# A graph layer on one core: a transposition moved on TensorE, two waits moved to ScalarE, a full-height last chunk and an earlier first message

## The reference, cut to what matters

```
h   = relu(layernorm(x))                       # x: 50000 x 128, float32
xn  = layernorm(h) * g1 + b1
msg = relu(xn[src] + edge_attr)                # 25000 edges, sorted by dst
aggr = segment_sum(msg, dst, 50000)
u   = (1 + eps) * xn + aggr
u   = relu(u @ Wg1 + bg1) @ Wg2 + bg2          # the GIN part, 128 -> 128 -> 128
h2  = h + u
f   = gelu(layernorm(h2)*g2+b2 @ Wf1 + bf1) @ Wf2 + bf2    # 128 -> 512 -> 128
out = x + h2 + f
```

## Time and profile before

| | |
|---|---|
| three runs, us | 1043.13, 1045.61, 1047.68 |
| profiled execution, us | 1042.96 |
| its span, us | 1041.2 |
| TensorE busy | 982.8 us, 94% |
| VectorE busy | 965.1 us, 93% |
| ScalarE busy | 852.8 us, 82% |
| GpSimd busy | 825.9 us, 79% |

### The profile page before, as it was taken

How to read it: one execution, slowest core, us unless ns; L and a number is a source line. 1 busy time by engine, 2 the same in 40 slices (tenths; PEclk the granted TensorE clock), 3 DMA queues, 4 the chain that set the end, 5 groups by cost and what they waited for, 6 DMA issues and landing times. The chain is left out here.

```text
span 1041.2 us, 23085 instructions
## 1 busy us (share of the span) xinstructions
PE 982.8 (94%) x6684; PEld 857.0 (82%) x6684; DVE 965.1 (93%) x3499; ACT 852.8 (82%) x2158; POOL 825.9 (79%) x510
## 2 busy tenths in 40 slices
PE   1569999999999999999999999999999999999978
PEld 0357888988889889889888889889889889888867
DVE  5979999999999999999999999999999999998642
ACT  1458888898888988988888988988988988978853
POOL 7788888888788888888888888888888888876610
PEclk9869999999999999999999999999999999999999
DMA  7856766877886654555654664654654554543221
GB/s 259 228 165 162 204 172 179 242 230 220 253 238 157 160 130 118 157 133 117 156 135 116 154 139 116 157 136 115 158 134 116 150 140 117 125 105 81 51 60 41
DMA packets 110468, 156.87 MB, mean 151 GB/s; under 512 B 24835, under 2 KB 50607, under 8 KB 110334
## 3 DMA queue, kind: packets, MB, share of 16 engines
q1 hardware_dynamic: 70358, 128.99, 39.0%
q0 software_dynamic: 37760, 25.66, 17.7%
q10 hardware_dynamic: 2216, 0.66, 0.3%
HBM read 90.61 MB, written 64.61 MB: 149 GB/s over the span
## 5 line engine op out<-in xcount | busy, mean ns | idle before, releaser
L451 POOL DMA_INDIRECT aggr_sums<-e_merged,e_index x196 | 339.2, 1731 | 80.6 <-issue 70.7
L939 PE MATMUL p_out<-wf,n_act 128*128 128x128 f32 x3136 | 370.5, 276 | 1.6
L939 PEld LDWEIGHTS p_out<-wf,n_act 128*128 128x128 f32 x3136 | 357.7, 191 | 6.9 <-DVE p_out L855 5.9
L460 POOL TENSOR_TENSOR n_rstd<-n_var,minus_half 128x16 f32<-128x16 f32 (+3 forms) x102 | 259.7, 2557 | 48.3 <-DVE n_var L835 32.2
L532 ACT ACTIVATE n_act<-p_f,bf1e_col 128x512 f32<-128x512 f32 x392 | 256.2, 680 | 35.2 <-PE p_f L902 31.3
L440 POOL DMA_INDIRECT e_x<-in_x,e_cols x196 | 223.2, 1139 | 61.0 <-issue 59.4
L902 PE MATMUL p_f<-n_z2T_high,wf_low 128*128 128x512 f32 x392 | 202.0, 515 | 5.6 <-DVE n_z2T_low L701 4.8
L902 PE MATMUL p_f<-n_z2T_high,wf_high 128*128 128x512 f32 x392 | 155.1, 396 | 0.0
L902 PE MATMUL p_f<-n_z2T_low,wf_high 128*128 128x512 f32 x392 | 154.6, 394 | 0.0
L687 DVE BATCH_NORM_STATS2 n_stat<-n_x 128x6 f32<-128x256 f32 x392 | 140.3, 418 | 0.6 <-issue 0.4
L614 ACT ACTIVATE n_inT<-p_in 128x512 f32<-128x512 f32 x98 | 58.5, 597 | 99.0 <-PE p_in L946 99.0
(11 more groups left out here) (85 smaller groups left out, 1455.4 us busy)
## 6 DMA issues: line engine op xcount, KB each, us to landing
n_x<-in_x SPq DMA_DIRECT2D x97, 256.0 KB, 3.0
n_aggr<-aggr_sums SPq DMA_DIRECT2D x97, 256.0 KB, 2.7
out_dram<-n_out SPq DMA_DIRECT2D x97, 256.0 KB
aggr_sums<-zeros SPq DMA_DIRECT2D x26, 512.0 KB, 5.2
e_dst<-in_dst_rows SPq DMA_DIRECT2D x49, 256.0 KB, 3.8
e_attr<-in_attr SPq DMA_DIRECT2D x48, 256.0 KB, 3.5
aggr_sums<-zeros SPq DMA_DIRECT2D x12, 1024.0 KB, 5.7
e_x<-in_x,e_cols POOLq DMA_INDIRECT x196, 3.7
```

The source lines that it names most:

```text
L451: nc.gpsimd.indirect_dma_start(out=aggr, out_offset=bass.IndirectOffsetOnAxis(ap=e_index[0:r, s, j:j + 1], axis=0), in_=e_merged[0:r, s, j ...
L460: return nc.gpsimd.tensor_tensor(n_rstd[0:r, s, lo:hi], n_var[0:r, s, lo:hi], minus_half[0:r, 0:(hi - lo) * J].rearrange("p (a j) -> p a j ...
L939: last = nc.tensor.matmul(p_out[0:b.rows, j, :], n_act[:, k, j, 0:b.rows], wf2[:, k, :], start=False, stop=(k == KF - 1), skip_group_check ...
```

## The change

- On TensorE the transposition of z2 now stands between `p_g` and FFN1's quarters 2 and 3, not behind them.
- `merged_rows` on ScalarE takes over two waits of GpSimd in the branch that is taken: for the zeroed parts of `aggr_sums` and for the scatters of the chunk before. GpSimd's wait for `s_eindex` goes too.
- The last chunk's gathers and scatters always take 128 partitions. VectorE first fills the chunk's index rows from 96 on with spare rows beyond the sums (one copy of 32 partitions by 4), then writes the 106 true ones.
- `FIRST_JOINED` is 2: the powers of chunks 2 and 3 go into those of blocks 0 and 2 (in column 2, where nothing else stands so early), so those two node powers are 12 columns wide instead of 8, and two powers of their own disappear.
- In the prologue ScalarE makes a chunk's message one step earlier (`messages(edge(2))`); there, that is chunk 0.

```diff
-        FIRST_JOINED = 4
+        FIRST_JOINED = LEAD - 1
+        def joined_column(c):
+            return 3 if block_beside(c) >= 3 else 2
...
             def gather(c, columns):
-                r, s = c.rows, c.slot(3)
+                s = c.slot(3)
...
-                        out=e_x[0:r, s, j, :], out_offset=None, in_=x,
+                        out=e_x[0:P, s, j, :], out_offset=None, in_=x,
...
             def scatter_pair(c, g):
-                            ap=e_index[0:r, s, j:j + 1], axis=0),
-                        in_=e_merged[0:r, s, j, :], in_offset=None,
+                            ap=e_index[0:P, s, j:j + 1], axis=0),
+                        in_=e_merged[0:P, s, j, :], in_offset=None,
...
                     pool.wait_ge(s_emerged, c.at + 1)
-                    pool.wait_ge(s_eindex, c.at + 1)
+                    if apart:
+                        pool.wait_ge(s_eindex, c.at + 1)
...
-                    if not apart:
-                        for q in s_zeroed[zeroed_for(c.k - 1) if c.k else 0:zeroed_for(c.k)]:
-                            pool.wait_ge(q, 32)
-                    if not c.is_number(0):
+                    if apart and not c.is_number(0):
                         pool.wait_ge(q_scatter[(c.k - 1) % 3], SCATTERED * (c.value + (c.k - 1) // 3 + 1))
...
-                    power(b.rows, b.slot(8), 0, 4 if with_chunk else 3 if together else 2).then_inc(s_nrstd, 1)
+                    power(b.rows, b.slot(8), 0, 2 + together + with_chunk).then_inc(s_nrstd, 1)
...
+            def messages(c):
+                if c is not None:
+                    act.wait_ge(s_esum, c.at + 1)
+                    reached(act, s_emm, c.at - 2)
+                    nc.scalar.activation(e_msg[0:c.rows, c.slot(3)], e_sum[0:c.rows, c.slot(3)],
+                                         ACT.Relu).then_inc(s_emsg, 1)
-            def merged_rows(c):
+            def merged_rows(c, apart):
                 if c is not None:
+                    if not apart:
+                        for q in s_zeroed[zeroed_for(c.k - 1) if c.k else 0:zeroed_for(c.k)]:
+                            act.wait_ge(q, 32)
+                        if not c.is_number(0):
+                            act.wait_ge(q_scatter[(c.k - 1) % 3], SCATTERED * ((c.k - 1) // 3 + 1))
                     act.wait_ge(s_emm, c.at + 1)
...
-                if 0 in halves and (c := edge(3)) is not None:
-                    act.wait_ge(s_esum, c.at + 1)
...
+                if 0 in halves and not alone(node, apart):
+                    messages(edge(3))
+                elif 1 in halves and alone(node, apart):
+                    messages(edge(2))
...
+                    if r < P:
+                        lo = r // 32 * 32
+                        nc.vector.tensor_copy(e_index[lo:P, s], spare[lo:P]).then_inc(s_spare_rows, 1)
+                        dve.wait_ge(s_spare_rows, 1)
...
-                if (b := seventh) is not None:
-                    first_product(b, (2, 3))
                 if (b := sixth) is not None:
                     pe.wait_ge(s_z2, b.at + 1)
                     reached(pe, s_z2T_low, b.at)
                     ...
                     last.then_inc(s_tz2, 1)
+                if (b := seventh) is not None:
+                    first_product(b, (2, 3))
```

More of the change, by code:

```diff
@@ L219, in gnn_kernel @@
              "order_in", "bounds", "order", "bad", "flag"))
+        s_spare_rows = sem("s_spare_rows")
         s_zeroed = [sem(f"s_zeroed{i}") for i in range(len(ZERO_PARTS))]
@@ L440, in gather @@
                     nc.gpsimd.indirect_dma_start(
-                        out=e_x[0:r, s, j, :], out_offset=None, in_=x,
-                        in_offset=bass.IndirectOffsetOnAxis(ap=e_cols[0:r, s, 0, j:j + 1], axis=0),
+                        out=e_x[0:P, s, j, :], out_offset=None, in_=x,
+                        in_offset=bass.IndirectOffsetOnAxis(ap=e_cols[0:P, s, 0, j:j + 1], axis=0),
                         bounds_check=bound,
@@ L497, in step @@
                     if with_chunk:
-                        assert together and block_beside(c) == b.k
+                        assert together == (joined_column(c) == 3) and block_beside(c) == b.k
                         pool.wait_ge(s_evar, c.at + 1)
-                    power(b.rows, b.slot(8), 0, 4 if with_chunk else 3 if together else 2).then_inc(s_nrstd, 1)
+                    power(b.rows, b.slot(8), 0, 2 + together + with_chunk).then_inc(s_nrstd, 1)
                 if ending is not None and not together:
@@ L575, in step @@
                 if 1 in halves and 0 not in halves and (c := edge(3)) is not None and not c.is_number(0):
-                    merged_rows(c)
+                    merged_rows(c, apart)
                 if (b := node(0)) is not None:
@@ L587, in step @@
                     gelu(b, 3)
-                if 0 in halves and (c := edge(3)) is not None:
-                    act.wait_ge(s_esum, c.at + 1)
-                    reached(act, s_emm, c.at - 2)
-                    nc.scalar.activation(e_msg[0:c.rows, c.slot(3)], e_sum[0:c.rows, c.slot(3)],
-                                         ACT.Relu).then_inc(s_emsg, 1)
+                if 0 in halves and not alone(node, apart):
+                    messages(edge(3))
+                elif 1 in halves and alone(node, apart):
+                    messages(edge(2))
                 if (b := node(5)) is not None:
@@ L774, in second_half @@
                     dve.wait_ge(s_estatu, c.at + 1)
-                    to = n_var[0:r, block_beside(c) % 8, 3] if joined(c, apart) else e_var[0:r, s, 1]
+                    to = n_var[0:r, block_beside(c) % 8, joined_column(c)] if joined(c, apart) else e_var[0:r, s, 1]
                     nc.vector.scalar_tensor_tensor(to, e_stat[0:r, s, 1, :, 2], 1.0 / D, e_var[0:r, s, 0],
@@ L799, in sum_of @@
                         dve.wait_ge(s_nrstd, block_beside(ending) + 1)
-                        rstd = n_rstd[0:r, block_beside(ending) % 8, 3]
+                        rstd = n_rstd[0:r, block_beside(ending) % 8, joined_column(ending)]
                     else:
```

## The result

Three rounds on one chip, each kernel in turn: after 1034.43 us (median of 6 runs, 1033.29 to 1037.35), before 1046.46 us (6 runs, 1043.13 to 1047.77). The ratio is 0.9891, with a 95% interval from 0.9872 to 0.9911: 11 to 12 us faster, with an interval from 9.3 to 13.4. The profiled execution of after took 1033.71 us, span 1031.9; that of before 1042.96 and 1041.2. Between the two profiles lie only 9.3 us, since the one of before was among its fastest runs.

A forecast was written before the change was run, and what follows sets the result against it. VectorE and the loop of power, scatters, landing and load of sums bound the middle; the last chunk's slow scatters, the end. 7.0 + 2.1 + 0.85 + 1.5 = 11.4 us less gave 1034, range 1029 to 1039.5.

The forecast's parts named there:

- Part 1: Last chunk's scatters on 128 partitions land like the others; the 16.0 us step returns to 9.0: 7.0 us less.
- Part 2: Last chunk's gathers on 128 partitions: VectorE's n_in near 909 us no longer waits for late sums, 2.1 us less.
- Part 3: Transposition of z2 on TensorE: hidden in waits of three of the last steps, 0.85 us less; nothing in the middle.
- Part 4: Prologue: earlier message and joined powers bring forward gathers VectorE awaits near 57 and 75 us; 1.5 us less.
- Part 5: Two waits moved from GpSimd to ScalarE's e_merged: cost 0, and GpSimd's saved time goes unused, so 0.
- A: Last chunk's scatters stay slow, their landing due to its rows or the program's end: 1043 us; chance 0.07.
- B: Middle gets faster too, through GpSimd's saved time (1028 us) or the weight loads' waits (1013 us); chance 0.08.
- C: ScalarE is held by the moved wait, slower than before: 1086 us at 1.1 us in each of 47 pairs; chance 0.04.
- D: The tail's gain comes, but prologue and gathers give nothing: 1038 us; chance 0.11.

The follow-up runs named there:

- last chunk alone: The kernel before with 128 partitions in the last chunk's gathers and scatters, and the copy of spare rows, alone: 1031.77 us, ratio 0.9908.
- waits alone: The kernel before with the two waits moved from GpSimd to ScalarE's e_merged and GpSimd's wait for s_eindex removed: 1042.76 us, ratio 1.0005.
- order alone: The kernel before with only the transposition of z2 moved ahead of FFN1's quarters 2 and 3: 1040.79 us, ratio 0.9991.
- prologue alone: The kernel before with only the powers of chunks 2 and 3 joined to the blocks' and chunk 0's message a step earlier: 1041.25 us, ratio 0.9997.
- scatters 128: The kernel before with 128 partitions in the last chunk's scatters only, its gathers still on 106: 1038.24 us, a single run.
- 112: The kernel after with 112 partitions instead of 128 in the last chunk's gathers and scatters: 1035.47 us, a single run.
- 122: The kernel after with 122 partitions instead of 128 in the last chunk's gathers and scatters: 1044.96 us, a single run.
- one zero later: The kernel after with one zeroing transfer put off by a step, the one at 35.8 us instead of the intended one at 50.4: 1035.48 us.
- attributes 128: The kernel after with the last chunk's loads of e_attr and e_cols over 128 partitions too: 1035.05 us, ratio 0.9881 to the kernel before.

## Why the prediction was right

The forecast was 1034 and the measured median is 1034.43. The likeliest case was the one that came, and the parts priced at 9.95 of its 11.45 us measured 10.2 below. The last 1.5, the prologue's, aren't borne out. Without them the same sum gives 1035.7, which the measurement doesn't tell from 1034.2 either; that the total fits to half a microsecond is luck.

One pair of profiles can't price parts of 1 to 2 us: between before and the last chunk alone, which run the same code in the middle, the middle alone differs by 5.0 us (766.79 and 761.80). The experiments give several profiles for each side of every part, so the steps are read as means between fixed points: VectorE's first read of gathered rows (e_stat), and the starts of TensorE's `p_g` in steps 7, 90 and 98 (us from the span's start):

```
                 prologue  gathers  transp.  scatters   e_stat   step 7  step 90  step 98  span
before           old       106      old      106         14.63    89.81   906.28   984.91  1041.2
waits alone      old       106      old      106         15.36    91.21   905.21   983.74  1040.9
order alone      old       106      new      106         15.38    91.04   902.93   982.43  1039.0
prologue alone   new       106      old      106         14.49    88.71   903.92   982.60  1039.2
scatters 128     old       106      old      128         15.33    91.35   907.76   987.09  1036.4
last chunk 128   old       128      old      128         15.23    91.10   902.70   979.80  1029.2
after            new       128      new      128         14.42    89.37   906.02   983.36  1031.9
112              new       112      new      112         14.51    89.82   908.43   985.20  1033.7
122              new       122      new      122         14.23    89.28   906.25   985.86  1043.2
one zero later   new       128      new      128         14.56    89.60   908.34   985.25  1033.7
attributes 128   new       128      new      128         14.15    88.82   904.31   981.09  1029.7
```

(In the second row the start of step 7 is taken from the end of its `p_g`, whose first part the trace lacks.)

- **Part 1, the last chunk's scatters: 7.0 predicted.** From step 98 to the end, old order: 56.29, 57.16 and 56.60 us with 106, 49.31 and 49.40 with 128. Means 56.68 and 49.36: **7.3**. The mechanism held at each point: the landing took 3.4 us at most for the 3.8 assumed, n_in came at 985.27, TensorE did not wait. The slowest landing of the earlier trace rows (7.0), the lower bound's, did not come. That the partitions are the cause was an estimate, from this chunk's being the one on 106; the runs with 112 and 122 show it (3.1 us at most and 8.05). That same 7.0 speaks against one reason given: "no other of the 192" scatters was slow isn't so, since one in the middle took as long as chunk 48's.
- **Part 2, its gathers: 2.1 predicted.** From step 90 to step 98: 78.63, 78.53, 79.50, 78.68 and 79.33 with 106, and 79.61 with 122; 77.10, 77.34, 76.77, 76.91 and 76.78 with 128 or 112. Means 79.05 and 76.98: **2.1**. The pair of profiles had shown 1.3 over this stretch and 1.6 over the one step. The copy of the spare rows takes 0.36 us (at 932.47 in after), for the 0.3 that was kept, and costs nothing that is seen. The size held, the path only in part. In before and in the waits alone the loads of the sums land late, after up to 4.8 and 5.0 us, and n_in waits 2.20 and 2.35. With 128 or 112 they take 3.2 at most, and n_in's wait in after is 0.54 (at 909.30). But with 122 no load beside the gathers took more than 3.1, and the time was lost to the gathered rows themselves:

```profile
922.73 0.77 DVE L701 BATCH_NORM_STATS2 e_stat<-e_x 106x6 f32<-106x256 f32 x2 [2.50 <-DMA e_x<-in_x,e_cols]
```

  The same wait is 1.98 us in the order alone and 1.22 with the scatters on 128; it doesn't appear with 128 or 112. The prediction had no term for it. GpSimd's issues of the chunk's gathers also take 1.64 to 1.70 us with 106 and 1.75 to 1.81 with 122, for 1.04 to 1.26 in after, and what that adds isn't separated.
- **Part 3, the transposition: 0.85 predicted.** From step 98 to the end with fast scatters: 49.31 and 49.40 old; 48.54, 48.50, 48.45 and 48.61 new. Means 49.36 and 48.52: **0.8**. In the middle nothing, as argued: a wait of 0.3 us of the weight loads was one that TensorE's 1.39 us groups covered. Beside the slow scatters the same span shows no gain (56.57 and 57.34 with the new order), but the gain is there. From the start of the next step's FFN2 to the end of the last one it is 32.37 to 32.39 us in all five kernels with the old order, and 31.53 to 31.58 in all six with the new. What covers it is the stretch ahead of that FFN2, behind TensorE's standstill (5.23 us in before, 4.88 in the order alone, 4.87 and 5.17 in the prologue and the waits alone, 6.42 with 122): from p_in it takes 7.20 us in before, 7.80 and 8.07 in the prologue and the waits alone, 7.91 with 122 and 8.46 in the order alone, and 5.41 in after, where nothing stood still. The granted clock over it was 0.76 in before and 0.65 in the order alone, and `p_g` took 0.86 us there in before, 1.39 to 1.71 in the other four. So before's own profile had the least of this loss, and from it alone part 1 is 6.9.
- **Part 4, the prologue: 1.5 predicted, not seen at the end.** Up to step 7: 89.81, 91.21, 91.04, 91.35 and 91.10 old, mean 90.90; 88.71, 89.37, 89.82, 89.28, 89.60 and 88.82 new, mean 89.27: 1.6 less, the size predicted. Half of that isn't the change's: VectorE has its first gathered rows at 15.19 on average in the old kernels and at 14.39 in the new ones, 0.8 earlier, before anything of the change has run; no run shows why. From there to step 7 it is 75.72 old and 74.87 new: **0.8 less**. Nor did the gain come where it was predicted, as waits at e_stat that are shorter by 1.3 and then 1.5 us in all. These waits have means of 3.72 (near 58 us) and 2.27 (near 76) old, 3.78 and 2.33 new: no shorter. The rows do land earlier, at 56.84 for 58.25, but VectorE comes to the wait as much earlier, at 53.06 for 54.53. (Before's own profile, with 57.08, is the earliest of the old ones; that is why after's 57.09 looks unmoved.) The step also said "VectorE is the busy engine from there to the middle, so its 1.5 us stay", and that isn't borne out: alone it measured 0.3 us, with an interval from 1.8 faster to 1.1 slower, and step 90 starts at 904.98 on average with the old prologue and 906.21 with the new. This is the one term of the sum that the runs leave unsupported, though the interval doesn't exclude it. GpSimd's power doesn't lengthen VectorE's work where before's trace lets one compare: n_zg takes 1.13 us at 506.38, inside the power of 2.94 us at 506.18, and e_zg, of the same shape, 1.13 at 500.79, beside no power. The wider node powers take 2.35 us for 1.80 to 1.84, as counted.
- **Part 5, the two waits: 0 predicted.** Measured 1.0005 [0.9993, 1.0016], and ScalarE waits once, in the prologue, 2.2 us in after. GpSimd's 9 us fewer busy went unused in the middle, as said.

**Where the prologue's gain goes** is open in part. What the length of the middle (from 139 us to step 90) goes with is plain. VectorE's waits there, in the kernel with the shortest middle (the last chunk alone, 761.80 us):

```profile
DVE n_in L869 <- DMA n_aggr<-aggr_sums: 0.9, 4, 0.3
```

and in the one with nearly the longest (one zero later, 768.88 us):

```profile
DVE n_in L882 <- DMA n_aggr<-aggr_sums: 8.0, 16, 1.1
DVE n_in L882 <- POOL n_rstd L465: 1.1, 2, 0.6
```

The waits for the sums go with the length in all: 0.9 us of waits and 761.80; 2.7 and 762.16; 3.6 and 765.61; 3.9 and 763.88; 4.6 and 765.46; 5.1 and 766.92; 5.7 and 766.45; 5.8 and 766.90; 6.6 and 766.79; 7.3 and 769.18; 8.0 and 768.88. About 1 us of time for each. VectorE's busy time is between 758.9 and 759.9 in all of them. So VectorE's work is the floor and its waits for the loop's landings are what lies on it, as the prediction had it. With the new prologue the waits are somewhat longer on one chip (4.6 against 0.9, 2.7 and 3.9), and two of three are on another (7.3, 8.0 and 5.8 against 5.7); but between before and after they are not (6.6 and 5.1). Whether an earlier start makes the loop wait more, or the executions differ by chance, the runs don't tell.

**Rivals.** A (the landing has to do with the chunk's place or data) fell with 128 and 112 fast, 122 slow. B (the middle faster) fell: 766.79 and 766.92. C (ScalarE held) did not come, but its price is real: the same wait placed earlier costs 42 us, 1.1 us for each of the 37 pairs in which it is met. It is 1.5 us long there, so about three quarters of it reach the time, where the rival had counted all. D (prologue and gathers give nothing) is half true: the gathers gave 2.1, the prologue nothing that can be told at the end. The prediction's other check, e_stat's waits shorter by 1 us, came out wrong, and the total hid it.

## What to carry to other kernels

A short last chunk isn't a cheap one: look at the landings of an odd-sized tile by themselves, and if they are as slow as those of 106 or 122 partitions here (6.9 to 8.1 us, against 3.4 at most with 112 and 128), try the heights that were fast, by padding the transfer and not only the computation. A wait may be moved to an engine that is awaited only if the landing's whole distribution lies ahead of it; 4.4 us further up the same queue the same wait cost 4%. And a gain in the first microseconds is not one at the end: where a loop of transfers sets the pace, take part sizes as means over several profiles between fixed points, and begin them where the change first acts.

## What the runs showed of the hardware

- A scatter that adds, one row of 128 floats for each partition. In the last chunk, with 128 or 112 partitions, GpSimd needs 1.5 to 1.6 us to issue it and it lands in 3.4 us at most; with 106 it needs 2.7 to 3.0 in before and up to 3.4 in the waits alone, and lands in 6.9 to 7.6 and in up to 8.0; with 122 it needs 2.9 to 3.0, and the two landings in the chain took 7.7 and 8.1. (In the middle full ones took 3.2 to 7.0, median 3.8.) It moves 864 packets with 106 partitions, 992 with 122, 144 with 128 and 128 with 112.
- Slow gathers cost about 2 us here in either of two ways: a load of the sums beside them lands after 4.8 us instead of 2.7, or VectorE waits for the gathered rows (2.50 us with 122).
- After TensorE had stood still for 5.23 us in before and 4.88 in the order alone, the granted clock over the next stretch was 0.76 and 0.65, and the stretch took 7.20 and 8.46 us, against 5.41 at 1.00 in after. Such a loss varies between executions and can cover a gain of 0.8 us.
- GpSimd is busy for only 79% of the time, and yet its order counts: one transfer, with its wait for two landings, put ahead of the power cost 35 us.
